# Moving sixteen spare SBUF columns from behind the state mixing weights to in front of them

## The reference

```python
xz = layernorm(x) @ w_in                       # 256 -> 2 x 512
xp, z = split(xz)
xc = silu(causal_conv(xp, conv_w, 4 taps) + conv_b)
h[t] = 0.9 * h[t-1] + 0.1 * (xc[t] @ w_B)      # state of 16
y = (h @ w_C) * silu(z)
x = x + y @ w_out
n = layernorm(x)
# two of eight experts for each sequence, chosen by its first token
x = x + mean over the two of (gelu(n @ W1 + b1) @ W2 + b2)
```

## The kernel before

| tile | loaded as weights for | start, modulo 512 bytes |
|---|---|---|
| `w_in_hi`, `w_in_lo`, `w1_hi`, `w1_lo` | 512-column matmuls | 0 |
| `b_mix`, `c_mix` | 512-column matmuls | 0 |
| `y_hi`, `y_lo`, `hid_hi`, `hid_lo` | 256-column matmuls | 64 |
| what streams (`xn`, `xc`, `state_mix`, `w_out`, `w2`) | | 0 |

## Time and profile before

### The profile page before, as it was taken

The page is one execution under the profiler, slowest core; times in us unless marked ns, Lnnn a source line. Parts: engine busy times, 40 slices in busy tenths (PEclk is TensorE's granted clock), DMA queues, the critical chain, the costliest instruction groups (busy, mean ns, idle before and its releaser), DMA issues.

```text
span 507.5 us, 9839 instructions
## 1 busy us (share of the span) xinstructions
PE 503.0 (99%) x3026; PEld 447.6 (88%) x3026; DVE 452.3 (89%) x896; ACT 400.7 (79%) x692; POOL 348.2 (69%) x390
## 2 busy tenths in 40 slices
PE   8999999999999999999999999999999999999997
PEld 8889799898898989989899998989989899998997
DVE  6999899999998899989999899998999989996773
ACT  4986958878869788697887969779797887969454
POOL 4959597659693796928969197772977649673391
PEclk9999999999999999999999999999999999999999
DMA  8940005344251432606235170432604333130102
GB/s 266 292 174 12 32 0 173 119 131 162 74 182 37 165 124 83 206 17 193 79 124 165 42 223 24 165 124 86 203 40 143 106 125 125 51 115 0 43 3 83
DMA packets 53379, 57.28 MB, mean 113 GB/s; under 512 B 8682, under 2 KB 49642, under 8 KB 53226
## 3 DMA queue, kind: packets, MB, share of 16 engines
q1 hardware_dynamic: 51498, 56.67, 34.1%
q10 hardware_dynamic: 1856, 0.31, 0.3%
HBM read 35.46 MB, written 21.50 MB: 112 GB/s over the span
## 4 chain that ended last, share of the span: by engine, by line
PE 97%; DVE 1%; DMA 1%; issue 0%; DVEq 0%
PE blk L1291 16%; PE blk L1292 16%; PE blk L1296 16%; PE tok L1410 12%; PE tok L1408 12%; PE tok L1409 12%; PE turn L1449 3%; PE turn L1452 3%; PE blk L1471 3%; PE turn L1239 1%; PE tok L1291 1%; PE tok L1296 1%; PE tok L1292 1%; DMA x_mid<-in_L_attn_x 1%; DVE stats_t L914 0%; DVE normed L931 0%
## 5 line engine op out<-in xcount | busy, mean ns | idle before, releaser
L989 DVE SCALAR_TENSOR_TENSOR conv<-blk,tap_w,conv 128x512 f32<-128x512 f32 x192 | 130.1, 740 | 8.2 <-ACT conv L680 7.6
L485 POOL TENSOR_TENSOR y_lo<-gate,y_hi 128x512 fp32r<-128x512 f32 x57 | 72.2, 1299 | 36.6 <-ACT y_hi L608 36.5
L1291 PE MATMUL blk<-xn_hi,w_in_hi 128*128 128x512 f32 x228 | 89.5, 393 | 0.0
L1292 PE MATMUL blk<-xn_hi,w_in_lo 128*128 128x512 f32 x228 | 89.1, 391 | 0.0
L450 POOL TENSOR_TENSOR xc_lo<-conv,xc_hi 128x512 fp32r<-128x512 f32 x60 | 72.7, 1229 | 8.3 <-ACT xc_hi L608 8.1
L1408 PE MATMUL tok<-w_out_hi,y_hi 128*128 128x256 f32 x256 | 72.1, 282 | 0.0
L1410 PE MATMUL tok<-w_out_hi,y_lo 128*128 128x256 f32 x256 | 71.9, 281 | 0.0
L1409 PE MATMUL tok<-w_out_lo,y_hi 128*128 128x256 f32 x256 | 71.9, 281 | 0.0
L1296 PE MATMUL blk<-xn_lo,w_in_hi 128*128 128x512 f32 x228 | 70.3, 389 | 0.0
L1408 PE MATMUL tok<-w_hi,hid_hi 128*128 128x256 f32 x248 | 69.9, 282 | 0.0
L1410 PE MATMUL tok<-w_hi,hid_lo 128*128 128x256 f32 x248 | 69.7, 281 | 0.0
(11 more groups left out here) (189 smaller groups left out, 1321.7 us busy)
## 6 DMA issues: line engine op xcount, KB each, us to landing
spill<-normed SPq DMA_DIRECT2D x25, 512.0 KB, 2.8
normed<-spill SPq DMA_DIRECT2D x100, 128.0 KB, 2.8
out<-x_mid SPq DMA_DIRECT2D x30, 256.0 KB, 2.7
x_mid<-in_L_attn_x SPq DMA_DIRECT2D x29, 256.0 KB, 2.7
x_in<-in_L_attn_x SPq DMA_DIRECT2D x14, 512.0 KB, 4.3
w_all<-in_L_ffn_W SPq DMA_DIRECT2D x2, 2048.0 KB, 11.8
b_all<-in_L_ffn_b SPq DMA_DIRECT2D x1, 1024.0 KB, 13.1
gate<-in_L_attn_w_in SPq DMA_DIRECT2D x2, 256.0 KB, 4.5
```

What stands on the lines that cost most here:

```text
L485: nc.gpsimd.tensor_tensor(y_lo[:, j, :], gate_of(o, j), y_hi[:, j, :].bitcast(F32), ALU.subtract).then_inc(y_lo_set, 1)
L989: nc.vector.scalar_tensor_tensor(cols, blk[j][:], tap_w[:, j, t:t + 1], cols, ALU.mult, ALU.add).then_inc(tap_added, 1)
L1291: mm(dst, whi(k), his(k), start=(k == 0), stop=False)
L1292: mm(dst, wlo(k), his(k), start=False, stop=False)
```

## The change

The 16 spare columns are made in front of `b_mix` instead of behind `c_mix`. `b_mix` and `c_mix` move up by 64 bytes. Everything in front of them and everything behind them stays where it was, since the total is the same. No instruction is added, taken away or moved in the order; only the addresses in the instructions that read or write `b_mix` and `c_mix` differ.

```diff
         w1_hi, w1_lo = sb("w1_hi", [P, TOP_K, KD * D], F32R), sb("w1_lo", [P, TOP_K, KD * D], F32R)
+        behind_columns = sb("behind_columns", [P, 16])
         b_mix = sb("b_mix", [P, JD, P], F32R)
         c_mix = sb("c_mix", [P, DI], F32R)
-        behind_columns = sb("behind_columns", [P, 16])
         y_hi, y_lo = sb("y_hi", [P, JD, CH], F32R), sb("y_lo", [P, JD, CH], F32R)
```

## The result

The changed kernel takes 509.76 us (509.61 to 509.99, 20 runs) against 508.94 us for the kernel before (508.75 to 509.43, 20 runs). The ratio is 1.0016, with a 95% interval of 1.001 to 1.0022. It is slower by 0.82 us, within the 0.2% that the prediction called the same and in its range, but not the zero that it called likeliest.

What follows compares the result with a forecast made beforehand. The prediction took PE (TensorE) to bound the kernel. Its terms, 0 for the opening writes and 192 x 0 for the products, summed to 0 us on 509.06, so 509.1 us, with a range of 508.2 to 510.1 us.

Steps and rivals of the forecast that it cites:

- What bounds the kernel: Whole kernel: PE is busy 503.0 of 507.5 us at 2.4 GHz, so any change in matmul pitch lands one for one.
- The writes in the opening: ACT and POOL writes of `b_mix` and `c_mix` at the start: no change from the new addresses, zero us.
- The 192 products: 128 `b_mix` and 64 `c_mix` loads and products of 512 columns: pitch unchanged, 192 x 0 = 0 us (chance 0.50).
- the late `c_mix` products: Four `c_mix` products at 232.5 ns each, 6 ns over 226.3; as a bound on 192 products, 1.2 us more.
- The sign that the prediction named: Eight `b_mix` starts in PE's timeline: 1.81 us if unchanged, 1.79 for a small gain, 1.86 or more for a loss.
- The 14 ns of the other upper bound: First 512-column product behind a 256-column group, read as 0.24 us, 14 ns over; on 192 products, 2.7 us more.
- the loss rival: Slices at 64 straddle a multiple of 512, lengthening load and matmul on all 192: 509.8, or 510.2 to 511.8 us (0.09, 0.10).
- The number of products: All 192 products, 128 with `b_mix` and 64 with `c_mix`, were taken to pay any change of pitch.
- the 5.3 that the prediction set as the limit: Ns per product, over 192 products, at which the change passes 0.2% (1.02 us) and no longer counts as the same.
- the small loss: Under 5.3 ns more for each of the 192 products: 509.1 to 510.0 us, taken as 509.8; chance 0.09.
- the large one: A loss above 5.3 ns for each of the 192 products: 510.1 to 511.8 us; chance 0.10.
- The small constant gain: Fixed cost per product falls 2.3 ns at 512 columns as at 256: 0.44 us less, 508.6 us; chance 0.24.

## Why the prediction was right, and where it was not

- **What bounds the kernel: right.** The times moved one for one with PE's pitches, to the few tenths of a microsecond by which a profiled execution lies off its median. With everything at 0, 768 x 2.2 + 767 x 1.7 = 3.0 us from pitches met 3.0 us measured.
- **The writes in the opening: right at zero.** POOL's writes of `b_mix` took 323 ns in the changed kernel for 338, and those of `c_mix` 1291 for 1298.
- **The 192 products: the step that failed.** The prediction took zero because a load has 38 ns of room under 512 columns, so that a load a few ns longer or shorter would be hidden. The loads did stay at 188 ns. But the price isn't in the load. It shows in the product, 393 to 398 ns for 389 and 233.4 ns from start to start for 226.8, and there room for the load is no protection. The chosen row (load duration) was the wrong witness. The row whose size came out was that of the late `c_mix` products, named as an upper bound: 6 ns over, against 6.6 measured for `b_mix`. That both have one cause isn't shown. The sign that the prediction named did appear: eight `b_mix` products took 1.86 us.
- **The 14 ns of the other upper bound: a misreading.** It is the difference of two starts that are printed to 0.01 us. The trace has 233 ns there, 7 over 226.3 and not 14, so the loss rival's upper end of 511.8 us was too high.
- **The number of products: a third too many in the upper bound.** `c_mix` products already stood in such a disturbed stretch and paid nothing more. So it is 128 x 6.6 = 0.84 us and not 192 x 6.6 = 1.27. That the time stayed within 0.2% and in the range is in part luck: 6.6 ns a product is more than the 5.3 that the prediction set as the limit, and the sum stayed under the limit only because a third of the products didn't pay.
- **The loss rival: right in sign and near in size (509.8), wrong in mechanism.** The time fell where the small loss was put (0.09), the cost of a product where the large one was (0.10). The load didn't lengthen, and straddling a multiple of 512 costs nothing: with all at 64 the pitches are those of all at 0.
- **The small constant gain: wrong in sign at 512 columns.** That 64 goes together with 2.3 ns less at 256 columns was true and causal (117.9 to 120.1 ns with the offset taken away), but did not carry over to 512. The prediction had named this: "since then 256 columns tell little about 512".

## What to carry to other kernels

Where TensorE is the bound and weight loads run under streaming matmuls, the distance between the two operands' starts modulo 512 bytes is a knob to try. In this kernel it was worth 2 to 3% of the products' time, and its sign depended on the columns streamed. Here 0 (or 256) was best for 512 columns and 64 for 256 columns. Set it for each kind of product, and read the pitch from start to start, since the load's duration doesn't show it. A row for products of one length is no evidence for another length, and room to spare on one operand's side doesn't cover the other's.

## What the runs showed of the hardware

- For float32r products with a 128 x 128 load each, at a granted clock of 1.000: a steady 226 to 227 ns a product of 512 columns at distance 0 or 256, and 230 to 236 ns in alternation at 64, with 32 and 128 as dear on the mean; at 256 columns 120.0 ns at distance 0, and 117.7 at 64, 192 and 448.
- The page "TensorE: Matmul & The Clock Gate" of the Trainium skill, section "Step-by-step: what each phase is for", says that loading the next weights steals no SBUF read bandwidth from the running matmul, since each of the two has a read port of its own. Read as "the place of the weights can't matter to the matmul", as the prediction did, these runs disagree by up to 3%: moving the weights alone by 64 bytes lengthened the streaming product by 6.6 ns, and moving the streamed operand with them in all products took it back. Why, no run tells; whether the two meet in SBUF, and where, was not tried.
- At distance 64 a group of 256-column products has two steady rhythms, 117.7 and 113.4 ns. Which one it takes depends on what runs just before: moving `state_mix` alone turned the `hid` groups behind `c_mix`. It keeps it but for pauses: one, with 193 ns from start to start, turned a group in the kernel before. If all 1535 products ran at 113.4 it would be 6.6 us less (1.3%). How to bring every group into it stays open.
- A switch between 256 and 512 columns, or between distances, mostly disturbs some three to ten products of 512 columns, with differences of 224 to 238 ns, before the steady pitch is reached.
